# One PSUM bank moved from the query rows to the sums in a two-layer graph attention kernel

## The reference

```python
scores = jnp.einsum('ehd,ehd->eh', q[dst], k[src]) * scale
m = jax.ops.segment_max(scores, dst, num_segments=n)
ex = jnp.exp(scores - m[dst])
z = jax.ops.segment_sum(ex, dst, num_segments=n)
attn = ex / z[dst]
agg = jax.ops.segment_sum(attn[:, :, None] * v[src], dst, num_segments=n)
```

## Time and profile before

| what | value |
|---|---|
| median of three runs | 3921.0 us (3919.7 to 3940.48) |
| the profiled execution's own time | 3936.65 us |
| its span, first to last instruction | 3934.9 us |
| mean granted TensorE clock | 0.73 |
| busy: PE, DVE, ACT, POOL | 60%, 63%, 34%, 47% |
| work on edges, layer 0 and layer 1 | about 395 to 1645 us and 2136 to 3396 us of the span |

### The profile page before, as it was taken

How to read it: one execution, slowest core, us unless ns; L and a number is a source line. 1 busy time by engine, 2 the same in 40 slices (tenths; PEclk the granted TensorE clock), 3 DMA queues, 4 the chain that set the end, 5 groups by cost and what they waited for, 6 DMA issues and landing times. The chain is left out here.

```text
span 3934.9 us, 37573 instructions
## 1 busy us (share of the span) xinstructions
PE 2357.7 (60%) x7257; PEld 1558.8 (40%) x7258; DVE 2488.1 (63%) x3969; ACT 1327.4 (34%) x3895; POOL 1835.5 (47%) x1938
## 2 busy tenths in 40 slices
PE   6772555555554555478873555555555555388798
PEld 3331333333333333256552333333333333266676
DVE  3663887777777777643434777777777777544433
ACT  1111443443443444312112444444444434232131
POOL 4006566666666666221006666666666666111000
PEclk8775666666666666689995666666776666689899
DMA  2226676676667667412126666667676776312111
GB/s 92 84 64 198 186 213 209 208 208 207 206 204 209 204 207 211 136 49 86 62 70 203 200 208 208 203 210 207 208 212 210 210 209 208 99 54 66 40 36 33
DMA packets 293457, 623.34 MB, mean 158 GB/s; under 512 B 52005, under 2 KB 163805, under 8 KB 293284
## 3 DMA queue, kind: packets, MB, share of 16 engines
q0 software_dynamic: 149904, 471.38, 41.0%
q1 hardware_dynamic: 143380, 150.27, 11.9%
HBM read 526.62 MB, written 94.78 MB: 158 GB/s over the span
## 5 line engine op out<-in xcount | busy, mean ns | idle before, releaser
L710 POOL DMA_INDIRECT ring<-kv_table,stage_ix x1760 | 1673.5, 951 | 977.0 <-issue 588.2
L938 PE MATMUL bank<-qs,hot_q 128*128 x1760 | 716.7, 555 | 643.3 <-issue 365.6
L951 PE MATMUL bank<-ring,hot_w 128*128 128x272 f32 x1760 | 706.8, 541 | 500.5 <-issue 293.7
L1845 DVE TENSOR_TENSOR ring<-ring,bank 128x1024 f32<-128x1024 f32 x440 | 532.8, 1211 | 559.4 <-issue 331.4
L938 PEld LDWEIGHTS bank<-qs,hot_q 128*128 128x128 f32 x1760 | 463.6, 275 | 823.3 <-issue 726.3
L951 PEld LDWEIGHTS bank<-ring,hot_w 128*128 128x128 f32 x1760 | 419.7, 259 | 768.8 <-issue 505.7
L1850 DVE TENSOR_REDUCE s<-ring 128x32 f32<-128x1024 f32 x440 | 533.0, 1211 | 4.2
L1195 ACT ACTIVATE stage_o<-bank 128x272 f32<-128x272 f32 x440 | 167.5, 385 | 535.2 <-remote 320.9
L1180 ACT ACTIVATE s<-bank 128x8 f32<-128x8 f32 x440 | 78.1, 178 | 705.0 <-remote 467.3
L1170 ACT ACTIVATE hot_q<-pos_b,row_of 128x128 f32<-128x128 bf16 x880 | 304.2, 395 | 2.6
L1862 DVE TENSOR_TENSOR bank<-ring,bank 128x512 f32<-128x512 f32 x440 | 301.1, 684 | 0.0
(11 more groups left out here) (298 smaller groups left out, 2369.4 us busy)
## 6 DMA issues: line engine op xcount, KB each, us to landing
agg_d<-stage_o SPq DMA_DIRECT2D x440, 136.0 KB
ring<-kv_table,stage_ix POOLq DMA_INDIRECT x1760
pos_b<-rel_d SPq DMA_DIRECT2D x54, 256.0 KB
kv_table<-ring SPq DMA_DIRECT2D x50, 250.0 KB
h_dram<-ring SPq DMA_DIRECT2D x15, 625.0 KB
ring<-h_dram SPq DMA_DIRECT2D x15, 625.0 KB
ring<-in_x_dram SPq DMA_DIRECT2D x10, 625.0 KB
ring<-kv_table SPq DMA_DIRECT2D x10, 625.0 KB
```

What stands on the lines that cost most here:

```text
L710: gps.indirect_dma_start(out=chunk[:, par * G + i, j, :], out_offset=None, in_=table, in_offset=bass.IndirectOffsetOnAxis(ap=stage_ix[:, p ...
L938: mm = ten.matmul(q_bank(third, i)[:, 0:QC], hot_q[:, i % 4, a * P:(a + 1) * P], qs[:, bass.ds(t * QC + a * QC, QC)], start=(a == 0), stop ...
L951: mm = ten.matmul(b_acc[i % 2][:, lo - OWN:MC], hot_w[:, i % 4, :], chunk[:, s, j, lo:ROW], start=(j == 0), stop=(j == QD // 2 - 1), skip_ ...
L1845: tt(k_, k_, q, ALU.mult).then_inc(S["q_used"], 1)
```

## The change

The third bank of the query rows (bank 6) goes to the sums. Query rows are now made two blocks ahead of the block whose scores are done, and the sums of block n wait for the eviction of block n-3. The banks of the sums turn modulo 3 and those of the query rows modulo 2. On ACT the copy of the self scores moves from two blocks ahead to one block ahead, since the query rows are made later. At the start of a layer two blocks of query rows are made instead of three.

```diff
-        b_q, b_acc, b_two = (bank[0], bank[1], bank[6]), bank[4:6], bank[7]
+        b_q, b_acc, b_two = (bank[0], bank[1]), bank[4:7], bank[7]
@@
         def q_bank(third, i):
-            return b_q[(third * G + i) % 3]
+            return b_q[(third * G + i) % 2]
+
+        def acc_bank(third, i):
+            return b_acc[(third * G + i) % 3]
@@ PE
-                def sums(par, i, n, fresh=False):
+                def sums(par, third, i, n, fresh=False):
...
                     if not fresh:
-                        pe.wait_ge(S["evac"], n - 1)
+                        pe.wait_ge(S["evac"], n - 2)
...
-                        mm = ten.matmul(b_acc[i % 2][:, lo - OWN:MC], hot_w[:, i % 4, :], ...)
+                        mm = ten.matmul(acc_bank(third, i)[:, lo - OWN:MC], hot_w[:, i % 4, :], ...)
@@ PE, ahead
-                    if nn == G or i + 3 < nn:
-                        pe.wait_ge(S["hot_q"], n + 4)
+                    if nn == G or i + 2 < nn:
+                        pe.wait_ge(S["hot_q"], n + 3)
                         hold(pe, S["q_used"], n + 1, S["pe_passed"])
-                        queries(third, i + 3, t[i])
+                        queries(third, i + 2, t[i])
@@ PE, start of a layer
-                t = tiles_of(0, 3)
-                for x in range(3):
+                t = tiles_of(0, 2)
+                for x in range(2):
@@ ACT, evacuate
-                    sca.activation(stage_o[:, i % 4, :], b_acc[i % 2][:, 0:MC], ACT.Copy).then_inc(S["evac"], 1)
+                    sca.activation(stage_o[:, i % 4, :], acc_bank(third, i)[:, 0:MC], ACT.Copy).then_inc(S["evac"], 1)
@@ ACT, ahead
-                    if nn == G or i + 2 < nn:
-                        copy_self((par1 + (i + 2) // G) % 2, third + (i + 2) // G, (i + 2) % G, n + 2)
+                    if nn == G or i + 1 < nn:
+                        copy_self((par1 + (i + 1) // G) % 2, third + (i + 1) // G, (i + 1) % G, n + 1)
@@ ACT, start of a layer
-                for x in range(2):
-                    copy_self(0, 0, x, b0 + x)
+                copy_self(0, 0, 0, b0)
```

More of the change, by code:

```diff
@@ L947, in sums @@
                     if not fresh:
-                        pe.wait_ge(S["evac"], n - 1)
+                        pe.wait_ge(S["evac"], n - 2)
                     for j in range(QD // 2):
                         lo = OWN if j == 0 else D
-                        mm = ten.matmul(b_acc[i % 2][:, lo - OWN:MC], hot_w[:, i % 4, :], chunk[:, s, j, lo:ROW], start=(j == 0), stop=(j == QD // 2 - 1), skip_group_check=True)
+                        mm = ten.matmul(acc_bank(third, i)[:, lo - OWN:MC], hot_w[:, i % 4, :], chunk[:, s, j, lo:ROW], start=(j == 0), stop=(j == QD // 2 - 1), skip_group_check=True)
                     mm.then_inc(S["agg"], 1)
@@ L965, in ahead @@
                     n = k1 * G + (b0 + i)
-                    if nn == G or i + 3 < nn:
-                        pe.wait_ge(S["hot_q"], n + 4)
+                    if nn == G or i + 2 < nn:
+                        pe.wait_ge(S["hot_q"], n + 3)
                         hold(pe, S["q_used"], n + 1, S["pe_passed"])
-                        queries(third, i + 3, t[i])
+                        queries(third, i + 2, t[i])
                 def step(k, par, tk, tn, first, nk, nn, third):
                     if nn:
-                        t = tiles_of((k + 1) * G + 3, G if nn == G else nn - 3)
+                        t = tiles_of((k + 1) * G + 2, G if nn == G else nn - 2)
                     maxima(k, nk, 1)
                     if not first:
-                        sums(1 - par, G - 3, k * G + (b0 - 3))
+                        sums(1 - par, third - 1, G - 3, k * G + (b0 - 3))
                     maxima(k, nk, 2)
@@ L981, in step @@
                         for i in range(G - 2, G):
-                            sums(1 - par, i, (k - 1) * G + (b0 + i))
+                            sums(1 - par, third - 1, i, (k - 1) * G + (b0 + i))
                     for i in range(max(nn, G - 3)):
@@ L986, in step @@
                         if i < (G - 3 if nn else nk):
-                            sums(par, i, k * G + (b0 + i), first and layer == 0 and i < 2)
+                            sums(par, third, i, k * G + (b0 + i), first and layer == 0 and i < 3)
                 pe.wait_ge(S["q_in"], (layer + 1) * (NBATCH + 1) * 16)
-                t = tiles_of(0, 3)
-                for x in range(3):
+                t = tiles_of(0, 2)
+                for x in range(2):
                     hold(pe, S["hot_q"], b0 + x + 1, S["pe_passed"])
                     queries(0, x, t[x])
-                t = tiles_of(3, G)
+                t = tiles_of(2, G)
                 for i in range(G):
@@ L1188, in place, with evacuate @@
                     sca.activation(hot_w[:, i % 4, :], hot_w[:, i % 4, :], ACT.Relu, bias=ones[:, 0:1], scale=-1.0).then_inc(S["wpos"], 1)
-                def evacuate(k, i, n, fresh=False):
+                def evacuate(k, third, i, n, fresh=False):
                     if not fresh:
@@ L1221, in step @@
                     if not first:
-                        evacuate(k - 1, G - 4, n - 4)
+                        evacuate(k - 1, third - 1, G - 4, n - 4)
                     if nn:
@@ L1232, in step @@
                     if not first:
-                        evacuate(k - 1, G - 3, n - 3)
-                        evacuate(k - 1, G - 2, n - 2)
+                        evacuate(k - 1, third - 1, G - 3, n - 3)
+                        evacuate(k - 1, third - 1, G - 2, n - 2)
                     place(k * G + 1, 1, n + 1, virgin)
@@ L1242, in step @@
                             if i:
-                                evacuate(k, i - 1, n + (i - 1), virgin and i - 1 < 4)
+                                evacuate(k, third, i - 1, n + (i - 1), virgin and i - 1 < 4)
                             elif not first:
-                                evacuate(k - 1, G - 1, n - 1)
+                                evacuate(k - 1, third - 1, G - 1, n - 1)
                     if not nn:
-                        evacuate(k, nk - 1, n + nk - 1)
+                        evacuate(k, third, nk - 1, n + nk - 1)
                 act.wait_ge(S["pass_over"], layer + 1)
```

## The result

The changed kernel takes 3983.6 us (median of 4 runs, 3973.6 to 3995.5), the kernel before took 3930.7 us beside it. The ratio is 1.0144, 95% interval 1.0117 to 1.0171: slower by 53 us, where 242 us were forecast. The profiled executions say the same: spans of 3988.3 and 3934.9 us. The direction was right, the size was not: a group of eight blocks pays 1 us, not 4.5.

What follows compares the result with a forecast made beforehand. No engine was full on edges; late news of PE's finished work left DVE idle, waiting for query rows. Stalls 200 us, between stalls 42 and third bank 0 made 242 us over 3921.0: 4163 us, 6.2% slower, range 3965 to 4325.

Steps and rivals of the forecast that it cites:

- The stalls as a thing of their own: On edges, something holds PE's semaphores back about 17 us, whoever works next; DVE can do only blocks announced before.
- 50 x 4.0 = 200 us: DVE's scores: 50 stalls each leave one more block to do, 4.0 us apiece; bounds 125 and 400 us.
- 42 us between stalls: Between stalls, slow-clock PE makes DVE's scores 0.3 us late per block; half of 83 us taken, bounds 0 and 83.
- The third bank at 0: PE's sums: ending most of 118.3 us of eviction waits shortens nothing; taken as 0, bounds -118 and 0.
- The order of ACT at 0: ACT copies self scores one block later, 440 copies of 0.18 us as before; counted at 0.
- Lockstep: Rival, chance 0.11: both stall parts uncover DVE, or PE, ACT and DVE never catch up; 400 us more, 4321 us.
- Faster through the sums: Rival, chance 0.08: earlier sums free POOL's slots and PE's query rows; 3803 us at best, about 3860.
- Only the cheap block is lost: Rival, chance 0.14: stalls mostly uncover DVE at a group's end, 2.5 us a block; 60 to 125 us, about 4015.
- Nothing changes: Rival, chance 0.10: stall length follows PE's backlog, one block shorter, so the stall ends one block earlier; 3921 us.
- The signs of being wrong: Changed profile: stalls keeping 11 us, DVE waits not growing, or POOL gaining on waits for sums as much as the loss.

Runs made afterwards that it cites:

- e12: Kernel before with two of a block's four gathers issued after a layer's first two groups, chip A: 3346.8 us, one run, against 3928.5.
- e13: Kernel before with a 0.22 us memset on POOL behind each gather, chip A: 3936.2 us, one run, against 3928.5.
- e2: Kernel before with only ACT's copy of the self scores one block later, chip A: 3925.0 us, ratio 0.9991.
- e1: Changed kernel with two banks of sums instead of three, chip A: 3982.6 us against 3928.1 for the kernel before, ratio 1.0129.
- e10: Kernel before, unchanged, run once more on chip A: 3925.3 us.
- e11: Changed kernel, unchanged, run once more on chip A: 3980.8 us against 3928.5 for the kernel before, ratio 1.0134.
- e6: Kernel before with two of a block's four gathers issued after a layer's first two groups, chip B: 3306.9 us against 3523.2.
- e7: Changed kernel with two of a block's four gathers issued after a layer's first two groups, chip B: 3363.3 us.
- e15: Changed kernel with a memset on POOL behind each gather, chip C: 3676.3 us; the kernel before with the same memset took 3674.3.
- e18: Changed kernel, unchanged, on chip D: 3523.0 us against 3519.8 for the kernel before, ratio 1.0002.
- e8: Kernel before with a 0.22 us memset on POOL behind each gather, chip B: 3675.0 us against 3523.2, ratio 1.0426.
- e5: Kernel before with each gather after a layer's first two groups fetching a quarter of a row, chip A: 3912.7 us, one run, 0.4% faster.

## Why the prediction was wrong in its size

*The stalls as a thing of their own: failed.* The prediction read from the earlier trace rows "that the holding doesn't depend on who works next", and of POOL "32 of them are 40 us a group, under the 45". The first is wrong, and the second counts the gathers at the pace of their issue alone. The news is late only while POOL gathers: take half of the gathers away and the stalls go (e12), issue them slower and the time stays (e13). A group in the steady part of a layer is the gathers at the pace of chip A, 32 x 1.47 = 47 us; the prediction's 45 came from spreading a stretch, its ends included, over 28 groups. The row that said so was among those shown: POOL stood 4.28 us after its run, and the prediction says only that it "runs on through it".

*"50 x 4.0 = 200 us": the failed term.* It priced a block that DVE has still to do when the stall ends. Its count is somewhat high (40 waits over 6 us, not 50), but above all its price is wrong: the stalls grew by 1.5 us each at the first pair and by 0.7 at the second, and not even the added waiting is added time. The time of a group isn't DVE's work plus a stall of fixed length. It is close to the pace of the gathers, and DVE's stall is what is left over. e2 shows it, with 50 us more of these waits and no more time. In the changed kernel DVE's waits for scores rose by 105 us and its waits in the chain for the news of PE fell by 61, from 132.7 to 71.9, while the span rose by 53. The chain's first, before and then after:

```profile
DVE f_lane L1890 <- remote: 95.3, 10, 31.6
...
DVE f_lane L1890 <- PE bank L958: 37.4, 7, 10.4
```

```profile
DVE f_lane L1892 <- remote: 52.2, 17, 13.6
...
DVE f_lane L1892 <- issue: 19.7, 1, 19.7
```

That a block which DVE loses before a stall takes its place within POOL's next run is how I read it; no run shows it apart.

*What the 53 us are: in part argued.* e1 shows that they are the lookahead's, with 430.6 us of POOL's waits for sums. These waits rose by 54.0 us at the first pair and by 48 at e10 and e11, beside spans up by 53.4 and 55.8. POOL's runs became more: 137 before, 172 after, by its timeline, and the pace went from 1.47 to 1.50 us a gather, from 47.1 to 48.0 us a group. At 1.3 us for each of 35 more runs, less the 0.3 us that lie between any two gathers, this is 35 us, an estimate. How many long runs were cut depends on what counts as a break: with every break over 0.6 us, runs of 20 gathers went from 24 to 10, with breaks over 1.5 us alone from 30 to 31. So most of the added breaks are short, 0.6 to 1.5 us. That the lost block makes them is argued; no run changed the length of POOL's runs and nothing else.

*"42 us between stalls" (0 to 83): in its range where it can be seen.* 56 us of time and 51 us of DVE's waits where DVE is the bound and no stall covers any (e6, e7), where the same working gives 83; nothing where POOL is (e15, e18). How much of the 53 us on chip A it is, no run shows, so that 53 lies near 42 is no success of that term.

*The third bank at 0: right.* e1 equals the changed kernel; PE's 118.3 us of waits for evictions cost nothing. *The order of ACT at 0: right* (e2).

*The rivals.* Lockstep did not happen, and PE's granted clock did not fall: it is 0.70 in both edge stretches, against 0.68 before. Faster through the sums is refuted by e1. "Only the cheap block is lost" came nearest in number, with 60 us at its lower end, but by luck: it prices DVE's work behind a stall as the forecast does, only lower, and falls by the same runs. "Nothing changes" was nearest in mechanism: the length of the stall does follow a backlog, though as far as the runs show POOL's and not PE's. It was given 0.10, with the note that nothing in the rows showed it. Fewer gathers would have shown it, by an edit of two lines.

*The signs of being wrong.* None of the three that the prediction named came up as it stood: the stalls grew, DVE's waits grew, POOL's waits for sums grew instead of shrinking. DVE's busy share should have fallen to 0.69 and fell to 0.74.

## What to carry to other kernels

When an engine idles in a stage where nobody is full, find the engine whose work comes in unbroken runs that end where the idling ends, and ask what it costs until it is worked off, not only issued. Before pricing a stall per block, ask what the stage's time would be if the stall's victim had nothing to do; if it would be the same, lost lookahead is nearly free, as it was here. And time a change on more than one chip: here it is 1.4% on one and nothing on another.

## What the runs showed of the hardware

- The same kernel takes 3.93 ms on chip A and 3.52 ms on B, C and D, with POOL's gather at 0.95 us on each. On A a gather comes each 1.47 us on average in the steady part of a layer, on D each 1.25 (e18) and on B, when spaced, each 1.34 (e8), the pace of its issue. With half the gathers A and B are 1.2% apart (3346.8 and 3306.9 us). What differs between the chips isn't known.
- On A, while POOL gathers without a break, PE's finished matmuls are seen up to 14 us late (from 1019.15 to 1033.37 in the kernel before), and with half the gathers such waits go (e12); not all are, since a sum passed in the middle of a run at 1024.28.
- The bytes of a gather hardly matter: a quarter of them gave 0.4%, in one run on A (e5). The Trainium skill, in DMA: Bandwidth & Descriptors, section SWDGE vs HWDGE vs iDMA, says that GpSimd's gathers have their descriptors written by software into rings that the DMA engines drain. That would fit a pace set by gathers and not by bytes, but no run here looked into a ring.
